# Perceiver block on one core: the shift of the context rows as tensor times scalar, the division of outputs moved next to the second clamp, GpSimd's first two key sums ahead of deviations

## The chip, the cores and the metric

The kernel runs on one core of one Trainium2 chip. The core has five engines with queues of their own: TensorE (PE in the profile; its weight loads are PEld), VectorE (DVE), ScalarE (ACT), GpSimd (POOL), and SyncE (SP), which here only issues transfers. They meet at semaphores. The metric is the device time of one execution in microseconds: 1367.38 us, the median of three runs of the kernel before (1366.13, 1367.38 and 1373.22 us).

## The reference, cut to what matters

The block takes 16 sequences of 64 latents of width 256 and a context of 1024 rows of width 256 for each sequence, and applies three residual layers. All is float32.

```
# 1. cross attention, 16 heads of 64:       what this case is about
ctx = layer_norm(context) * ln_ctx_g + ln_ctx_b
q = layer_norm(latents) @ Wq
k, v = split(ctx @ Wkv)                       # 1024 rows, 16 heads of 64
k = [k1 * cos - k2 * sin, k2 * cos + k1 * sin]
attn = softmax(clip(q k^T / 8, -11, 11))
x = x + (attn v) @ Wo + bo
# 2. causal linear attention with relu features, 3. eight experts, two for each token
x = x + linear_attention(layernorm(x))
x = x + experts(layernorm(x))
```

The change touches the first layer alone.

## The kernel before, in words

The cross attention works on 128 steps: 16 sequences by 8 steps, and a step `j` is half of one sequence's context (512 rows) against a pair of head pairs. `two_steps(j)` on VectorE and on TensorE issues two steps; four steps share one output, so that two calls make a cycle, called a quad here: a call with `j % 4 == 0` and one with `j % 4 == 2`. There are 32 quads. Every order is written out by hand; nothing is planned by a program.

TensorE, in a call for `j`: in every second call `outputs` (L1627, 64 small matmuls, into the banks that the keys use too), then `scores(j)` and `scores(j + 1)` (L1561, 64 small matmuls each), `keys(j + 4)` (L1575, 12 matmuls of 512 columns), `sums(j - 2)` (L1604, 12), `keys(j + 5)`, `sums(j - 1)`. `outputs` waits until VectorE has taken the last keys out of the banks (`ku_done`, 8 n + 24). `keys` waits for the same of the step before, `scores` for the finished keys of GpSimd (`kr_done`), `sums` for the low parts of the weights (`p_lo_done`).

VectorE, in a call: `blocks_turned` (L1077, a 32 by 32 transpose of context rows), `added` (L1090, every second call), `shifts(j)` (L1060), `counted(j)` (L1068 and L1070, mean and variance of a tile of context rows), `clamped(j)` (L1082, the clip of the exponentials), `keys_turned(j)` (two times L1114 and L1115: keys out of PSUM times sine and times cosine), `clamped(j + 1)`, `weights_low(j)` (L1102, `p_lo = pr - p_hi`), `blocks_turned(j)`, and in every second call `divided` (L1096, `qo = o_part * lsum`) and `inverted` (L1086), then `shifts(j + 1)`, `counted(j + 1)`, `keys_turned(j + 1)`, in every second call `half_low` (L1124), and `weights_low(j + 1)`.

GpSimd, in a step: `keys_summed(j)` (L593, the cosine part plus the swapped sine part, 128 x 1024 elements, both read from SBUF), `deviations(j)` (L601 and L603, the reciprocal standard deviation of a tile) and `rows_low(j)` (L609). `keys_summed(j)` waits for `p_lo_done` of step `j - 1`: it may start as VectorE ends that step's `weights_low`.

ScalarE exponentiates (L773), rounds (L778), copies `o_part` (L787) and applies `rstd` and `shift` to the context rows (L739). The swapped sine part `ksw` comes from `kw` by four transfers of SyncE (L448).

`shift` is a column of 128 numbers: minus the mean times the reciprocal deviation. Steps below 0 are the lead-in, written out call by call for VectorE and as a loop from -5 for GpSimd.

Of the kernel before, what the change touches and what calls it, by code (L numbers as in the profile page):

```python
# [20 lines left out]
ALU = mybir.AluOpType  # L21
# [39 lines left out]
def build(nc, x, ctx_1024, cos, sin, lat_g, lat_b, ctx_g, ctx_b, Wq, Wkv, Wo, bo, Wqkv, bqkv, Wout, bout, proj,  # L61
          Wg, W1, b1, W2, b2, out):
    with ExitStack() as ctx:
        def sem(name):
            return ctx.enter_context(nc.semaphore(name))

        def sb(name, shape, dt=F32, scope=ctx):
            return scope.enter_context(nc.sbuf_tensor(name, shape, dt))
# [9 lines left out]
        mv = sb("mv", [P, 2, 2])  # L78
        ve = sb("ve", [P, 2])
        rstd = sb("rstd", [P, 2])  # L80
        shift = sb("shift", [P, 2])
# [189 lines left out]
        stats_done, rstd_done, shift_done, xhat_done = (sem(n) for n in ("stats_done", "rstd_done", "shift_done", "xhat_done"))  # L271
# [12 lines left out]
        def wait(eng, s, count):  # L284

            if count > 0:
                eng.wait_ge(s, count)

        def there(j):
            return 0 <= j < STEPS  # L290

        def due(j, first):

            return j >= first and (j - first) % 4 == 0 and (j - first) // 4 < QUADS
# [32 lines left out]
        def kr_at(j):  # L327

            return (kr_third[:], kr[:, 0], kr[:, 1], kr_fourth[:])[j % 4]
# [21 lines left out]
        def quad_cols(n):  # L351

            return n // 2 * N, n % 2 * 4
# [202 lines left out]
        def _(pool):  # L556
# [30 lines left out]
            def keys_summed(j):  # L587
                if there(j + 2):
                    i = j % 2
                    pool.wait_ge(ku_done, 2 * (j + 3))  # L590
                    wait(pool, p_lo_done, j)
                    pool.wait_ge(sw_ld[i], ((j + 2) // 2 + 1) * 64)
                    pool.tensor_tensor(kr_at(j + 2), kr_at(j + 2), ksw[:, i], ALU.add).then_inc(kr_done, 1)  # L593
# [11 lines left out]
            def rows_low(j):  # L605
                if there(j + 4):
                    n, t = tile_at(j + 4)
                    pool.wait_ge(x_hi_done, j + 5)
                    pool.tensor_tensor(xc[:, n, 1, t, 0:D - 1], raw[:, (j + 4) // ST % 2, (j + 4) % ST, 0:D - 1], xc[:, n, 0, t, 0:D - 1].bitcast(F32),  # L609
                                       ALU.subtract).then_inc(x_lo_done, 1)  # L610
# [16 lines left out]
                pool.wait_ge(rstd_done, (2 * c + 1) * ST // 2)  # L627
                pool.tensor_tensor(xl_rsd[:, t], xl_vpe[:, t], consts[:, 2:3].to_broadcast([P, ST // 2]), ALU.pow).then_inc(rstd_done, ST // 2)
            constants()
            for j in range(-5, 0):  # L630
                deviations(j)
                rows_low(j)
                keys_summed(j)
            for j in range(STEPS):
                keys_summed(j)
                deviations(j)
# [378 lines left out]
        def _(dve):  # L1015
# [38 lines left out]
            def shifts(j):  # L1054
                for n in stats_at(j - 1):
                    i = n % 2
                    dve.wait_ge(rstd_done, 2 * (n + 1))
                    if n >= ST + 2:
                        dve.wait_ge(xhat_done, n - 1)
                    dve.scalar_tensor_tensor(out=shift[:, i:i + 1], in0=mv[:, i, 0:1], scalar=-1.0, in1=rstd[:, i:i + 1],  # L1060
                                             op0=ALU.mult, op1=ALU.mult).then_inc(shift_done, 1)

            def counted(j):
                for n in stats_at(j):
# [14 lines left out]
            def clamped(j):  # L1079
                if there(j):  # L1080
                    dve.wait_ge(exp_done, j + 1)
                    dve.tensor_scalar(step_part(pr, j), step_part(pr, j), LOW, HIGH, ALU.max, ALU.min).then_inc(clamp_done, 1)  # L1082
# [9 lines left out]
            def divided(n):  # L1092
                at, g = quad_cols(n)
                dve.wait_ge(o_sum, 2 * n + 2)
                dve.wait_ge(lsum_ld, 64 * n + 64)
                dve.tensor_tensor(qo[:, g:g + 4, at:at + N], o_part[:].rearrange("p (g n) -> p g n", n=N),  # L1096
                                  lsum[:].rearrange("p (g n) -> p g n", n=N), ALU.mult).then_inc(o_done, 1)

            def weights_low(j):
                if there(j):  # L1100
                    dve.wait_ge(p_hi_done, j + 1)
                    dve.tensor_tensor(step_part(p_lo, j), step_part(pr, j), step_part(p_hi, j).bitcast(F32), ALU.subtract).then_inc(p_lo_done, 1)  # L1102
# [23 lines left out]
            def two_steps(j):  # L1126
                blocks_turned(j - 1)
                if due(j, 8):
                    added((j - 8) // 4)
                shifts(j)  # L1130
                counted(j)
                clamped(j)
                keys_turned(j, 0)
                keys_turned(j, 1)
                clamped(j + 1)
                weights_low(j)
                blocks_turned(j)
                if due(j, 10):
                    divided((j - 10) // 4)
                if due(j + 1, 7):  # L1140
                    inverted((j - 6) // 4)
                shifts(j + 1)
                counted(j + 1)
                keys_turned(j + 1, 0)
                keys_turned(j + 1, 1)
                if half_written(j - 1):
                    half_low(half_written(j - 1))
                weights_low(j + 1)
# [171 lines left out]
            for j in range(0, STEPS, 2):  # L1320
# [10 lines left out]
                if j >= STEPS - 6:  # L1331
# [3 lines left out]
                    i = (j - STEPS + 6) // 2  # L1335
# [690 lines left out]
```

## Time and profile before

| | |
|---|---|
| time, median of three | 1367.38 us |
| the profiled execution | 1373.17 us, span of its instructions 1371.4 us |
| granted TensorE clock, mean | 0.954 of 2.4 GHz |
| busy: PE, DVE | 1231.1 us (90%), 1156.1 us (84%) |
| busy: ACT, POOL | 653.0 us (48%), 605.3 us (44%) |
| cross attention in steady state | 124 to 1016 us of the span, 27 quads |

The profiled execution is one of the slower ones. A row of the timeline begins with the start in us from the span's start and the duration; in square brackets stands how long the engine sat idle before it and what ended that. Busy time of an instruction runs from its start to its end, and holds any time in which it was held. Rows of a busy engine overlap a little, since the next instruction starts before the last has drained.

### The profile page before, as it was taken

What the parts mean: (1) busy time and instruction counts of PE and PEld (TensorE: products, weight loads), DVE (VectorE), ACT (ScalarE), POOL (GpSimd) and SP (SyncE); (2) the same over time, 40 slices, a digit from 0 to 9 for tenths busy, and PEclk for the clock granted to TensorE, in tenths of its full rate; (3) what the DMA queues carried; (4) which work ended last, traced back from release to release, by engine and by line L of the source; (5) the groups of instructions that cost most, each with busy time, mean ns of one, the idle gap of its engine ahead of it and who ended that gap; (6) DMA issues with size and microseconds to landing.
All of it is one profiled execution on the core that took longest, in us unless ns stands there. A gap on an engine that the chain in (4) does not pass through costs nothing.

```text
span 1371.4 us, 39825 instructions
## 1 busy us (share of the span) xinstructions
PE 1231.1 (90%) x16268; PEld 1036.8 (76%) x16268; DVE 1156.1 (84%) x1954; ACT 653.0 (48%) x1089; POOL 605.3 (44%) x611
## 2 busy tenths in 40 slices
PE   7888898988988989888898888988999999999997
PEld 3677777777767767767777777777778888789997
DVE  6799989998989998999889898888986736757886
ACT  7454444444444444444444444444544423346664
POOL 2455544454544444554444454444444313332333
PEclk9999999999999999999889898999999999999999
DMA  5365555555555555555456554555456371366662
GB/s 208 82 151 129 126 125 129 131 120 121 120 121 121 124 128 124 132 131 129 122 123 126 120 122 119 124 126 119 121 146 134 90 223 64 102 189 203 190 191 82
DMA packets 136173, 181.36 MB, mean 132 GB/s; under 512 B 30316, under 2 KB 96312, under 8 KB 135864
## 3 DMA queue, kind: packets, MB, share of 16 engines
q1 hardware_dynamic: 110552, 150.80, 43.4%
q10 hardware_dynamic: 21360, 23.80, 6.8%
q0 software_dynamic: 4080, 4.22, 1.5%
q8 instruction: 129, 2.11, 0.7%
q14 instruction: 52, 0.43, 0.1%
HBM read 81.93 MB, written 30.56 MB: 82 GB/s over the span
## 4 chain that ended last, share of the span: by engine, by line
DVE 49%; PE 39%; issue 7%; ACT 2%; DMA 2%; POOL 1%; SPq 0%; POOLq 0%; DVEq 0%; ACTq 0%
PE bank L1575 9%; DVE shift L1060 9%; DVE p_lo L1102 7%; PE bank L1561 7%; DVE kw L1114 6%; PE bank L1930 5%; DVE kr L1115 5%; DVE pr L1082 5%; DVE qo L1096 5%; PE bank L1627 4%; PE bank L1604 3%; DVE ct L1124 2%; DVE xt L1077 2%; DVE bst L1068 2%; DVE kr_fourth L1115 2%
## 5 line engine op out<-in xcount | busy, mean ns | idle before, releaser
L1575 PE MATMUL bank<-ct,wk_hi 128*128 128x512 f32 x1024 | 335.0, 409 | 5.9 <-DVE kr_third L1115 2.9
L1604 PE MATMUL bank<-p_hi,xc 128*128 128x512 f32 x1024 | 316.1, 390 | 0.0
L1575 PEld LDWEIGHTS bank<-ct,wk_hi 128*128 128x128 f32 x1024 | 190.0, 193 | 55.7 <-DVE kr L1115 8.7
L1114 DVE TENSOR_TENSOR kw<-bank,stab 128x512 f32<-128x512 f32 x256 | 175.3, 685 | 60.8 <-PE bank L1575 58.2
L1604 PEld LDWEIGHTS bank<-p_hi,xc 128*128 128x128 f32 x1024 | 191.9, 188 | 39.8
L593 POOL TENSOR_TENSOR kr<-kr,ksw 128x1024 f32<-128x1024 f32 x64 | 153.7, 2403 | 123.4 <-issue 120.5
L778 ACT CAST p_hi<-pr 128x1024 fp32r<-128x1024 f32 x128 | 134.3, 1049 | 150.4 <-DVE pr L1082 150.4
L1575 PE MATMUL bank<-ct,wk_lo 128*128 128x512 f32 x512 | 202.9, 396 | 0.0
L1604 PE MATMUL bank<-p_lo,xc 128*128 128x512 f32 x512 | 199.2, 389 | 0.0
L773 ACT ACTIVATE pr<-bank 128x1024 f32<-128x1024 f32 x128 | 127.8, 1026 | 81.6 <-PE bank L1561 81.5
L1060 DVE SCALAR_TENSOR_TENSOR shift<-mv,rstd 128x1 f32<-128x1 f32 x120 | 162.5, 1354 | 0.0
L1102 DVE TENSOR_TENSOR p_lo<-pr,p_hi 128x1024 fp32r<-128x1024 f32 x128 | 156.1, 1219 | 0.6 <-ACT p_hi L778 0.5
L609 POOL TENSOR_TENSOR xc<-raw,xc 128x255 fp32r<-128x255 f32 x128 | 95.1, 743 | 125.7 <-ACT xc L748 125.7
L1627 PE MATMUL bank<-zt,wv 64*64 64x64 f32 x2048 | 49.8, 265 | 93.3 <-DVE kr_fourth L1115 90.3
L739 ACT ACTIVATE raw<-raw,shift,rstd 128x256 f32<-128x256 f32 x120 | 71.8, 600 | 121.8 <-DVE shift L1060 121.7
L1627 PEld LDWEIGHTS bank<-zt,wv 64*64 64x64 f32 x2048 | 45.2, 174 | 105.7 <-issue 105.7
L1082 DVE TENSOR_SCALAR pr<-pr 128x1024 f32<-128x1024 f32 x128 | 102.8, 803 | 19.2 <-ACT pr L773 19.2
L593 POOL TENSOR_TENSOR kr_third<-kr_third,ksw 128x1024 f32<-128x1024 f32 x32 | 76.8, 2399 | 94.4 <-issue 88.2
L593 POOL TENSOR_TENSOR kr_fourth<-kr_fourth,ksw 128x1024 f32<-128x1024 f32 x32 | 77.9, 2434 | 87.7 <-issue 80.7
L1575 PEld LDWEIGHTS bank<-ct,wk_lo 128*128 128x128 f32 x512 | 98.4, 192 | 23.1 <-issue 0.9
L1604 PEld LDWEIGHTS bank<-p_lo,xc 128*128 128x128 f32 x512 | 96.1, 188 | 20.1
L1561 PE MATMUL bank<-qo,kr 64*64 64x64 f32 x4096 | 87.8, 239 | 17.2 <-issue 12.6
(227 smaller groups left out, 2190.8 us busy)
## 6 DMA issues: line engine op xcount, KB each, us to landing
ksw<-kw SPq DMA_DIRECT2D x512, 128.0 KB, 2.3
x_turned<-xt SPq DMA_DIRECT2D x120, 128.0 KB, 2.5
ct_read<-x_turned SPq DMA_DIRECT2D x30, 512.0 KB, 4.9
w_two<-in_L_ffn_W_dram SPq DMA_DIRECT2D x15, 1024.0 KB
raw<-in_ctx_dram ACTq DMA_DIRECT2D x56, 256.0 KB, 3.4
x_slots<-fill ACTq DMA_DIRECT2D x32, 258.0 KB, 3.3
w_all<-in_L_ffn_W_dram SPq DMA_DIRECT2D x4, 2048.0 KB, 17.0
wo<-in_L_ffn_W_dram SPq DMA_DIRECT2D x7, 1024.0 KB, 5.0
```

Source lines behind the costliest of these rows:

```text
L593: pool.tensor_tensor(kr_at(j + 2), kr_at(j + 2), ksw[:, i], ALU.add).then_inc(kr_done, 1)
L773: act.activation(step_part(pr, j).rearrange("p (t h c) -> p h t c", h=2, c=P), heads[j % 2].rearrange("p h (t c) -> p h t c", c=P), ACT.Ex ...
L778: act.copy(step_part(p_hi, j), step_part(pr, j)).then_inc(p_hi_done, 1)
L1060: dve.scalar_tensor_tensor(out=shift[:, i:i + 1], in0=mv[:, i, 0:1], scalar=-1.0, in1=rstd[:, i:i + 1], op0=ALU.mult, op1=ALU.mult).then_i ...
L1082: dve.tensor_scalar(step_part(pr, j), step_part(pr, j), LOW, HIGH, ALU.max, ALU.min).then_inc(clamp_done, 1)
L1102: dve.tensor_tensor(step_part(p_lo, j), step_part(pr, j), step_part(p_hi, j).bitcast(F32), ALU.subtract).then_inc(p_lo_done, 1)
L1114: dve.tensor_tensor(by_tile(kw[:, i, cols]), keys_, by_tile(stab[:, places]), ALU.mult).then_inc(kw_done, 1)
L1115: dve.tensor_tensor(by_tile(kr_at(j)[:, cols]), keys_, by_tile(ctab[:, places]), ALU.mult).then_inc(ku_done, 1)
L1561: last = pe.matmul(banks[c * N:(c + 1) * N, h, t * 2 + a], kr_at(j)[rows, cols], qo[rows, g, at:at + N], start=True, stop=True)
L1575: last = pe.matmul(psK[:, a * 512:(a + 1) * 512], l[:, k, w], ct[:, h % 3, r, k], start=(m == 0), stop=(m == len(parts) - 1))
L1604: last = pe.matmul(psZ[c], xc[:, slot_, l, t, cols], r[:, i, :, t], start=(f == 0 and m == 0), stop=(f == 1 and m == len(parts) - 1), skip ...
L1627: last = pe.matmul(out_bank(n, r)[h * DH:(h + 1) * DH, i * N:(i + 1) * N], wv[rows, k, g * P + h * DH:g * P + (h + 1) * DH], zt[rows, k, ( ...
```

## The change

Three edits. In `shifts`, the product of the mean, -1 and `rstd` is no longer one operation of two tensors and a constant but one of a tensor, a scalar read per partition (`rstd`) and a constant. In `two_steps` of VectorE, `divided` goes from behind `blocks_turned(j)` to between `clamped(j + 1)` and `weights_low(j)`. In GpSimd's lead-in, `keys_summed(-2)` and `keys_summed(-1)` go ahead of their step's `deviations` and `rows_low`.

```diff
             constants()
-            for j in range(-5, 0):
+            for j in range(-5, -2):
                 deviations(j)
                 rows_low(j)
-                keys_summed(j)
+            keys_summed(-2)
+            deviations(-2)
+            rows_low(-2)
+            keys_summed(-1)
+            deviations(-1)
+            rows_low(-1)
...
-                    dve.scalar_tensor_tensor(out=shift[:, i:i + 1], in0=mv[:, i, 0:1], scalar=-1.0, in1=rstd[:, i:i + 1],
-                                             op0=ALU.mult, op1=ALU.mult).then_inc(shift_done, 1)
+                    dve.tensor_scalar(shift[:, i:i + 1], mv[:, i, 0:1], rstd[:, i:i + 1], -1.0, ALU.mult, ALU.mult).then_inc(shift_done, 1)
...
                 clamped(j + 1)
+                if due(j, 10):
+                    divided((j - 10) // 4)
                 weights_low(j)
                 blocks_turned(j)
-                if due(j, 10):
-                    divided((j - 10) // 4)
                 if due(j + 1, 7):
                     inverted((j - 6) // 4)
```

The first place is VectorE in the second call of a quad, from the second clamp to the last keys of the quad. `pr` is clamped there, `p_lo` is the low part of the weights, `xt` the turned rows, `qo` the divided output, `kw` and `kr_fourth` the keys' sine and cosine parts. Before:

```order
L1082 TENSOR_SCALAR pr<-pr 128x1024
L1102 TENSOR_TENSOR p_lo<-pr,p_hi 128x1024
L1077 STREAM_TRANSPOSE xt<-raw 128x8x32
L1096 TENSOR_TENSOR qo<-o_part,lsum 128x4x64
L1086 RECIPROCAL l_parts<-l_parts 128x4
L1060 SCALAR_TENSOR_TENSOR shift<-mv,rstd 128x1
L1068 BN_STATS bst<-raw 128x6
L1070 BN_AGGR mv<-bst 128x2
L1114 TENSOR_TENSOR kw<-bank,stab 128x512
```

The same place after; the edits above have moved the line numbers by 4 or 5:

```order
L1086 TENSOR_SCALAR pr<-pr 128x1024
L1100 TENSOR_TENSOR qo<-o_part,lsum 128x4x64
L1106 TENSOR_TENSOR p_lo<-pr,p_hi 128x1024
L1081 STREAM_TRANSPOSE xt<-raw 128x8x32
L1090 RECIPROCAL l_parts<-l_parts 128x4
L1065 TENSOR_SCALAR shift<-mv,rstd 128x1
L1072 BN_STATS bst<-raw 128x6
L1074 BN_AGGR mv<-bst 128x2
L1118 TENSOR_TENSOR kw<-bank,stab 128x512
```

`qo` stands two rows earlier, ahead of `p_lo` instead of behind it, and `shift` is a TENSOR_SCALAR.

The second place is GpSimd in the lead-in, steps -2, -1 and the sum of step 0. `ve` and `rstd` are the deviations, `xc` the low rows, `kr_third` and `kr` the keys of steps 0, 1 and 2. Before:

```order
L601 TENSOR_TENSOR ve<-mv,consts 128x1
L603 TENSOR_TENSOR rstd<-ve,consts 128x1
L609 TENSOR_TENSOR xc<-raw,xc 128x255
L593 TENSOR_TENSOR kr_third<-kr_third,ksw 128x1024
L601 TENSOR_TENSOR ve<-mv,consts 128x1
L603 TENSOR_TENSOR rstd<-ve,consts 128x1
L601 TENSOR_TENSOR ve<-mv,consts 128x1
L603 TENSOR_TENSOR rstd<-ve,consts 128x1
L609 TENSOR_TENSOR xc<-raw,xc 128x255
L593 TENSOR_TENSOR kr<-kr,ksw 128x1024 x2
```

The same place after:

```order
L593 TENSOR_TENSOR kr_third<-kr_third,ksw 128x1024
L601 TENSOR_TENSOR ve<-mv,consts 128x1
L603 TENSOR_TENSOR rstd<-ve,consts 128x1
L609 TENSOR_TENSOR xc<-raw,xc 128x255
L593 TENSOR_TENSOR kr<-kr,ksw 128x1024
L601 TENSOR_TENSOR ve<-mv,consts 128x1
L603 TENSOR_TENSOR rstd<-ve,consts 128x1
L601 TENSOR_TENSOR ve<-mv,consts 128x1
L603 TENSOR_TENSOR rstd<-ve,consts 128x1
L609 TENSOR_TENSOR xc<-raw,xc 128x255
L593 TENSOR_TENSOR kr<-kr,ksw 128x1024
```

Each of the first two sums stands three and five rows earlier; the third keeps its place behind `xc`.

## Rows read from the trace of the kernel before

**Rows 1.** Busy time by stretch, us and instructions: PE, PEld, DVE, ACT, POOL; clock, DMA.

```profile
124.00:1016.00 892.00, 788.26 (x11232) 654.33 (x11225) 807.82 (x1181) 413.71 (x592) 431.41 (x426) 0.94 0.53 125
...
585.69:617.46 31.77, 27.70 (x416) 22.67 (x417) 30.43 (x45) 15.43 (x22) 16.14 (x16) 1.00 0.58 130
1016.00:1043.19 27.19, 27.19 (x416) 22.71 (x416) 22.59 (x29) 13.22 (x18) 13.14 (x8) 1.00 0.67 147
...
92.00:124.00 32.00, 25.65 (x233) 20.17 (x234) 31.86 (x44) 12.98 (x19) 16.96 (x16) 0.93 0.48 113
```

**Rows 2.** Waits of PE, 60 to 1010 us: total, times, longest; one in the timeline.

```profile
PE bank L1627 <- DVE kr_fourth L1115: 88.7, 26, 3.5
...
553.41 1.99 PE L1627 MATMUL bank<-zt,wv 64*64 64x64 f32 x64 [3.41 <-DVE kr_fourth L1115]
```

**Rows 3.** Timeline of DVE over one quad.

```profile
538.09 1.21 DVE L1102 TENSOR_TENSOR p_lo<-pr,p_hi 128x1024 fp32r<-128x1024 f32 x1
...
539.59 2.26 DVE L1060 SCALAR_TENSOR_TENSOR shift<-mv,rstd 128x1 f32<-128x1 f32 x1
...
542.32 0.66 DVE L1082 TENSOR_SCALAR pr<-pr 128x1024 f32<-128x1024 f32 x1
...
547.65 2.52 DVE L1096 TENSOR_TENSOR qo<-o_part,lsum 128x256 f32<-128x256 f32 x1
...
550.18 0.12 DVE L1060 SCALAR_TENSOR_TENSOR shift<-mv,rstd 128x1 f32<-128x1 f32 x1
...
556.20 0.71 DVE L1060 SCALAR_TENSOR_TENSOR shift<-mv,rstd 128x1 f32<-128x1 f32 x1
```

**Rows 4.** Timeline of POOL over the same quad.

```profile
539.44 2.40 POOL L593 TENSOR_TENSOR kr_third<-kr_third,ksw 128x1024 f32<-128x1024 f32 x1 [3.21 <-issue]
...
547.50 2.39 POOL L593 TENSOR_TENSOR kr<-kr,ksw 128x1024 f32<-128x1024 f32 x1 [1.81 <-issue]
...
554.53 2.36 POOL L593 TENSOR_TENSOR kr<-kr,ksw 128x1024 f32<-128x1024 f32 x1 [2.08 <-issue]
```

**Rows 5.** Groups by line, 124 to 1016 us: busy us, mean ns, idle before.

```profile
L1060 DVE SCALAR_TENSOR_TENSOR shift<-mv,rstd 128x1 f32<-128x1 f32 x106 | 147.9, 1396 | 0.0
...
L1096 DVE TENSOR_TENSOR qo<-o_part,lsum 128x256 f32<-128x256 f32 x27 | 68.1, 2521 | 0.0
...
L1077 DVE STREAM_TRANSPOSE xt<-raw 128x256 f32<-128x256 f32 x108 | 46.9, 435 | 0.0
...
L1068 DVE BATCH_NORM_STATS2 bst<-raw 128x6 f32<-128x256 f32 x105 | 43.5, 414 | 0.0
```

**Rows 6.** Timeline of POOL and of DVE from 118 us.

```profile
118.17 2.40 POOL L593 TENSOR_TENSOR kr<-kr,ksw 128x1024 f32<-128x1024 f32 x1 [1.82 <-issue]
...
118.33 0.13 DVE L1086 RECIPROCAL l_parts<-l_parts 128x4 f32<-128x4 f32 x1
118.38 2.20 DVE L1060 SCALAR_TENSOR_TENSOR shift<-mv,rstd 128x1 f32<-128x1 f32 x1
```

**Rows 7.** Timeline of DVE where the context rows have run out.

```profile
1003.66 2.80 DVE L1082 TENSOR_SCALAR pr<-pr 128x1024 f32<-128x1024 f32 x1
...
1038.68 0.41 DVE L1096 TENSOR_TENSOR qo<-o_part,lsum 128x256 f32<-128x256 f32 x1
```

**Rows 8.** Groups of the whole span: a scalar per partition, and a constant.

```profile
L1170 DVE TENSOR_SCALAR raw<-raw,xl_mom,xl_rsd 128x256 f32<-128x256 f32 x8 | 2.7, 405 | 0.3 <-POOL xl_rsd L628 0.3
...
L1027 DVE TENSOR_SCALAR crep<-cs_raw 128x256 f32<-128x256 f32 x8 | 1.7, 286 | 2.3 <-DMA cs_raw<-in_L_xattn_sin_dram 2.3
```

**Rows 9.** Timeline of the lead-in: POOL, DVE and PE.

```profile
48.97 2.41 POOL L593 TENSOR_TENSOR kr_third<-kr_third,ksw 128x1024 f32<-128x1024 f32 x1
...
57.12 5.11 POOL L593 TENSOR_TENSOR kr<-kr,ksw 128x1024 f32<-128x1024 f32 x2
...
58.17 1.84 DVE L1082 TENSOR_SCALAR pr<-pr 128x1024 f32<-128x1024 f32 x1
...
59.60 1.99 PE L1561 MATMUL bank<-qo,kr 64*64 64x64 f32 x64 [4.63 <-POOL kr L593]
```

## The prediction

> **What bounds the kernel now.** I read the table of stretches first, then the waits of TensorE, then the timelines of VectorE and GpSimd over one quad. The steady part, 124 to 1016 us, holds 27 quads in 892 us, 33.04 us each [rows 1]. TensorE is busy 788 us of it and VectorE 808 us, so neither looks free. But of VectorE's busy time much is no work. `shift` is 128 numbers, one for each partition, and takes 1396 ns in the mean; free of any hold it takes 0.12 us [rows 3, 5]. `qo` takes 2521 ns against 0.41 us when free [rows 5, 7]. The reader is to see what GpSimd does meanwhile: its 2.40 us sum starts at 539.44, just behind the end of `p_lo` (538.09 and 1.21), and `shift`, started at 539.59, ends at 541.85, with that sum [rows 3, 4]. `qo` from 547.65 to 550.17 sits on the sum of 547.50 to 549.89 in the same way. So VectorE is held, in a quad, 4 x 1.396 - 4 x 0.12 = 5.1 us in `shift` and 2.1 us in `qo`, 7.2 us of 33.04.
>
> TensorE pays for that in one place: `outputs` waits for the last keys of the quad (`kr_fourth`), 88.7 us in 26 waits, 3.41 us each [rows 2]. In the quad at 585.69, with the clock at full rate all through, 31.77 us minus that wait are 28.4 us of nearly unbroken work. The quad at 1016.00 shows TensorE with no wait at all: 27.19 us for the same 416 matmuls, clock 1.00 [rows 1]. The rest of the 33.04 us, 2.4 us, is clock and small stalls: a mean of 0.94 with the levels 2.4 and 1.2 GHz is 12% of the stretch, 107 us, at 1.2 GHz; if TensorE worked through all of it that costs 53 us, 2.0 us in a quad. Some quads with the 3.4 us wait run at 1.00, those without a wait at 1016 all do.
>
> **The change, part by part.** The shift first. Its new form reads one tensor and a scalar per partition. The trace has no such instruction under a key sum, so I bound it by its neighbours. Below: a reciprocal of one small input runs 0.13 us from 118.33, inside the sum that started at 118.17, and the old `shift` right behind it is held 2.20 us by that same sum [rows 6]; so what matters is not that VectorE works at all, but what the instruction reads. Above: the old hold, 1.396 us in the mean. A scalar per partition costs something of its own, 405 against 286 ns on 256 columns [rows 8], 0.12 us. I take the value of the nearest row, free, about 0.15 us.
>
> What is late next, for each of the four shifts of a quad? Behind the one at 539.59 comes 0.6 us of statistics and then the clamp (542.32), a tensor against constants over 1024 columns, and that form does get held: 2.80 us instead of 0.66 at 1003.66 [rows 3, 7]. So this hold moves to the clamp and only 0.5 us is won. Behind the two shifts of the odd steps come statistics (0.6 us) and four halves of keys out of PSUM (about 2.4 us), none of them held in the trace; they cover the 2.4 us sum whole. One of these two is won entirely, 2.1 us; the other was already short (0.12 at 550.18), since `qo` had absorbed the sum before it. The one at 556.20 had 0.59 us, and ScalarE's exponentials are waited for just behind it: nothing.
>
> The division: at its new place, behind the second clamp, no key sum runs (the last ended at 541.84, the next starts behind `p_lo`), so it takes 0.41 us, and 2.1 us go, as long as the shift behind it is free too. `p_lo` and the sum that it releases come 0.34 us later; that sum then lies beside transpose, statistics and keys. Its wait for `lsum` costs nothing: that transfer is issued two steps before. Together VectorE's chain gets 0.5 + 2.1 + 2.1 = 4.7 us shorter in a quad, 28.3 us instead of 33.04, and the 2.0 us of slow clock that it also waits behind leave it as well once TensorE has no gap: 26.3 us. That is below 27.19 us, so TensorE becomes the bound. A second way gives the same: in the quad at 1016.00 VectorE is busy 22.59 us, without transposes, shifts and statistics; four transposes (0.44), four statistics (0.41 and about 0.1) and four shifts (0.15) add 4.4 us: 27.0 us, in which holds of the clamps are counted as work [rows 1, 5, 7]. So the margin is between 0.2 and 2 us, thin but positive, and it is the weak point of this forecast.
>
> A quad then costs 27.19 us and some stalls. The clean quad at 585.69 had 1.2 us of them, the whole part on the mean 2.4 - 2.0 = 0.4 us; I take 0.65, 27.84 us. 27 x (33.04 - 27.84) = 140 us. Ends: no stall, 158 us; 1.2 us of stalls and a remaining gap of 1 us, 99 us.
>
> The lead-in: `scores(1)` waits 4.63 us for the second sum, which stands behind deviations and rows and starts at 57.12; the clamp at 58.17 is held by it to 60.0 [rows 9]. With the sums ahead, the first starts one step of deviation and rows before 48.97, an estimate of 46.5, the second behind it and one such step, at about 50.5 us, and ends before 54.97, when TensorE begins to wait: `scores(1)` starts there instead of at 59.60, and the keys behind it no longer start after a pause. I take 7 us, between 4.6 and 8. From there to the first `outputs`, TensorE is idle 6.35 us of 92 to 124, and its clock of 0.93 costs another 2.2 [rows 1]; some of that is a rescaling of weights that stays on VectorE. I take 7.5 us, between 3 and 9.
>
> Sum: 140 + 7 + 7.5 = 155 us. The span of 1371.4 us becomes 1216, and the profiled execution's 1373.2 becomes 1218. That execution is 5.8 us above the median of the three runs; from the median the same sum gives 1212. I say 1214 us.
>
> The Trainium skill, SBUF — State Buffer, section Who interferes with whom, says that VectorE with two inputs in SBUF, or in one of its two-port modes, and a GpSimd instruction that reads SBUF exclude each other for a whole instruction, and that one with at most one SBUF input outside these modes never waits; rows 3, 4 and 6 agree for two inputs and for one. The page also counts the tensor-times-scalar form among those that may enter a two-port mode, which speaks against the edit: by that the new shift would be held as before, and the rival below gets its chance from it.
>
> **The rivals.** First, the change doesn't do what it says: the per-partition scalar is fetched the way a second tensor is, or a tensor times scalar is held like the clamp at 1003.66. Then each shift still ends with the sum, and the 2.1 us of the division are paid back by the shift two rows behind it. Only the lead-in's 7 us remain: 1360 us. For it speaks row 1003.66; against it that 256 columns with per-partition scalars take 405 ns and with a constant 286, so this form is not the fast one that the clamp is, and one column leaves nothing to split.
>
> Second, VectorE stays the bound. The margin above is thin, GpSimd's `rows_low` (two SBUF inputs) can now lie in front of the last `p_lo` of a quad, and a gap that only shrinks leaves the slow clock behind it: 28.3 + 2.0 = 30.3 us a quad, 27 x 2.7 = 74 us, with 10 from the start 84: 1283 us.
>
> Third, the gaps go but TensorE's clock still falls to 1.2 GHz 12% of the time: 27.84 + 2.0 us, 27 x 3.2 = 86 us and 12 from the start: 1269 us. Against it: after 1016 us, with no waits, the clock is 1.00.
>
> Slower: the held shift of the first rival with the price of its new form on top, 0.12 us [rows 8] on 120 shifts, all on VectorE's chain, 14 us, with the early sums in the lead-in holding VectorE there and winning nothing: 1381 us. It decides from the point where the new shift is held in most odd steps.
>
> **How the numbers follow.** TensorE-bound quads 0.68, VectorE still the bound 0.12, slow clock without gaps 0.08, shift held 0.07, slower 0.03, something else 0.02. The likeliest gives 1214 us, its own range 1196 to 1245. With the third case and half of the second the range reaches to 1275; the low end is the stall-free quad with the better ends of the start. What a measurement of this kernel can tell from no change is about 0.5%, 7 us. The first rival, at 1360, lies on that border and counts half and half: faster 0.93, same 0.04, slower 0.03.
>
> **What the profile after would show.** Right: `shift` at 0.1 to 0.2 us in the mean over all 120; `qo` at 0.4; the wait of `outputs` for `kr_fourth` gone or under 0.5 us a quad; starts of `outputs` 27.5 to 28.3 us apart; clock above 0.98; VectorE with several short waits for TensorE's keys; the mean of the clamp up from 0.80 to about 1.2 us, since it takes over holds; the second key sum ended by 53 us. Wrong: `shift` still above 1 us (first rival or the slower case), or an `outputs` wait of 1 to 3 us with VectorE busy through the quad (second), or a clock of 0.94 with no waits (third).

## The result, and the profile after

The changed kernel takes 1234.12 us in the median of 4 runs (1229.36 to 1237.52), the kernel before 1367.43 on the same chip: ratio 0.9015, 95% interval 0.8973 to 0.9058. The forecast was 1214 us, with 1196 to 1245 us for its likeliest case and a range that reaches to 1275. The profiled execution took 1237.52 us, its span 1235.8, and the sum is again made there.

The stretches first, to be set beside [rows 1]; the columns are the same.

```profile
111.66:879.06 767.40, 743.72 (x11233) 618.73 (x11233) 685.61 (x1181) 411.75 (x592) 434.27 (x427) 0.99 0.59 146
...
479.45:506.65 27.20, 27.20 (x418) 22.71 (x417) 25.35 (x45) 15.28 (x22) 16.16 (x16) 1.00 0.62 153
506.65:535.67 29.02, 27.34 (x418) 22.72 (x417) 25.36 (x45) 15.44 (x22) 16.16 (x16) 1.00 0.55 142
```

The first block of `outputs` starts at 111.66 us (before: 123.65), the 28th at 879.06 (before: 1016.00). Between them lie the same 27 quads, now in 767.40 us instead of 892.35, 28.42 each instead of 33.05 (33.04 in [rows 1], where the stretch starts at 124.00). A clean quad takes 27.20 us, with TensorE busy in all of it; VectorE has 25.35 us of work there, so 1.85 us of slack. The account: 892.35 - 767.40 = 124.9 us from the quads, 12.0 from the start, and 1.3 lost behind the start of the 28th outputs (355.4 us before, 356.7 after): 135.6 us, which is 1371.4 - 1235.8.

What TensorE waits for in the steady part (total us, times, longest), against [rows 2], and the chain that ended last, by engine:

```profile
PE bank L1565 <- issue: 21.7, 14, 2.1
PE bank L1579 <- issue: 1.9, 2, 1.7
```

```profile
PE 87%; DVE 4%; issue 3%; DMA 2%; ACT 2%; SPq 1%; POOL 1%; POOLq 0%; ACTq 0%; DVEq 0%
```

The wait of `outputs` for `kr_fourth`, 88.7 us before, is gone. What is left has no releaser: "issue" is idle time for which the profile shows no other engine. The chain is TensorE's at 87%.

The two instructions that were changed, over the whole span (ns: shortest, median, longest), against [rows 5]:

```profile
L1065 DVE TENSOR_SCALAR shift<-mv,rstd x120: 164/174/216, 36.3 to 861.2; 128x1 f32<-128x1 f32 x120
```

```profile
L1100 DVE TENSOR_TENSOR qo<-o_part,lsum x32: 410/413/426, 133.4 to 971.5; 128x256 f32<-128x256 f32 x32
```

And VectorE beside GpSimd in one quad, first VectorE, then GpSimd, against [rows 3, 4]:

```profile
495.01 0.17 DVE L1065 TENSOR_SCALAR shift<-mv,rstd 128x1 f32<-128x1 f32 x1
...
495.81 1.99 DVE L1086 TENSOR_SCALAR pr<-pr 128x1024 f32<-128x1024 f32 x1
...
500.97 0.41 DVE L1100 TENSOR_TENSOR qo<-o_part,lsum 128x256 f32<-128x256 f32 x1
501.30 1.21 DVE L1106 TENSOR_TENSOR p_lo<-pr,p_hi 128x1024 fp32r<-128x1024 f32 x1
...
502.86 0.17 DVE L1065 TENSOR_SCALAR shift<-mv,rstd 128x1 f32<-128x1 f32 x1
```

```profile
494.86 2.39 POOL L593 TENSOR_TENSOR kr_third<-kr_third,ksw 128x1024 f32<-128x1024 f32 x1 [2.35 <-DVE p_lo L1106]
...
502.65 2.41 POOL L593 TENSOR_TENSOR kr<-kr,ksw 128x1024 f32<-128x1024 f32 x1 [2.15 <-issue]
```

The shift at 495.01 lies inside GpSimd's sum of 494.86 to 497.25 and takes 0.17 us. The clamp that comes 0.8 us later is held to 497.80, just past the end of that sum: the hold has moved on, as the prediction said. The shift at 502.86 lies under the next sum and is followed by statistics and keys, none of which is held: here the whole 2.1 us are won. `qo` at 500.97 stands clear of both sums.

The lead-in, against [rows 9], GpSimd and then TensorE:

```profile
47.23 2.40 POOL L593 TENSOR_TENSOR kr_third<-kr_third,ksw 128x1024 f32<-128x1024 f32 x1
...
51.08 2.87 POOL L593 TENSOR_TENSOR kr<-kr,ksw 128x1024 f32<-128x1024 f32 x1
```

```profile
54.55 1.16 PE L1565 MATMUL bank<-qo,kr_third 64*64 64x64 f32 x64
55.53 1.11 PE L1565 MATMUL bank<-qo,kr 64*64 64x64 f32 x64
```

The second sum ends at 53.95, and `scores(1)` starts at 55.53 straight behind `scores(0)`, instead of at 59.60.

### The profile page after: what moved, and what is told of

Read it like the earlier page. It is cut to its first block, busy times and chain, and to the rows that moved or that the text cites. A ratio compares the mean times of both kernels' runs of the same rounds, so it can differ in the third digit from the quotient of the medians.

```text
span 1235.8 us, 39825 instructions
## 1 busy us (share of the span) xinstructions
PE 1183.8 (96%) x16268; PEld 998.4 (81%) x16268; DVE 1021.3 (83%) x1954; ACT 650.5 (53%) x1089; POOL 609.2 (49%) x611
## 3 DMA queue, kind: packets, MB, share of 16 engines
q8 instruction: 129, 2.11, 0.7%
## 4 chain that ended last, share of the span: by engine, by line
PE 87%; DVE 4%; issue 3%; DMA 2%; ACT 2%; SPq 1%; POOL 1%; POOLq 0%; ACTq 0%; DVEq 0%
PE bank L1579 29%; PE bank L1608 27%; PE bank L1565 10%; PE bank L1934 6%; PE bank L1631 3%; PE bank L1738 2%; PE bank L1984 2%; PE bank L1985 2%; PE bank L1986 1%; PE bank L1791 1%; PE bank L1815 1%; PE bank L1834 1%; DMA x_slots<-xn_all,slot 1%; DMA w_two<-in_L_ffn_W_dram 1%; PE bank L1824 1%
## 5 line engine op out<-in xcount | busy, mean ns | idle before, releaser
L1579 PE MATMUL bank<-ct,wk_hi 128*128 128x512 f32 x1024 | 328.6, 402 | 5.3 <-DVE kr_third L1119 3.1
L1106 DVE TENSOR_TENSOR p_lo<-pr,p_hi 128x1024 fp32r<-128x1024 f32 x128 | 169.0, 1321 | 0.5 <-ACT p_hi L783 0.4
L1086 DVE TENSOR_SCALAR pr<-pr 128x1024 f32<-128x1024 f32 x128 | 140.0, 1094 | 20.1 <-ACT pr L778 18.1
L694 POOL DMA_INDIRECT out_dram<-ys,result_no x23 | 51.4, 2236 | 98.7 <-DMA out_dram<-ys,result_no 74.3
L1565 PE MATMUL bank<-qo,kr 64*64 64x64 f32 x4096 | 76.8, 220 | 22.6 <-issue 22.6
L1565 PEld LDWEIGHTS bank<-qo,kr 64*64 64x64 f32 x4096 | 68.0, 135 | 35.7 <-issue 35.7
L735 ACT COPY zt<-bank 128x512 f32<-128x512 f32 x64 | 37.2, 582 | 95.7 <-PE bank L1608 95.7
L1119 DVE TENSOR_TENSOR kr<-bank,ctab 128x512 f32<-128x512 f32 x128 | 86.8, 678 | 0.0
```

Of the source, the lines that this page charges most:

```text
L1119: dve.tensor_tensor(by_tile(kr_at(j)[:, cols]), keys_, by_tile(ctab[:, places]), ALU.mult).then_inc(ku_done, 1)
L1565: last = pe.matmul(banks[c * N:(c + 1) * N, h, t * 2 + a], kr_at(j)[rows, cols], qo[rows, g, at:at + N], start=True, stop=True)
L1579: last = pe.matmul(psK[:, a * 512:(a + 1) * 512], l[:, k, w], ct[:, h % 3, r, k], start=(m == 0), stop=(m == len(parts) - 1))
```

## The experiments

All ratios are to the kernel before, run on the same chip; starts, quads and waits come from one profiled execution of each kernel. The times of before there were 1365.23 us (first four kernels), 1368.96 (the next four), 1364.06 (three) and 1366.02 (the last).

**The parts of the change.** Four kernels carry it in pieces. Edit 1 is the shift's form, edit 2 the place of the division, edit 3 the order of GpSimd's first sums.

```diff
# edit 1
-                    dve.scalar_tensor_tensor(out=shift[:, i:i + 1], in0=mv[:, i, 0:1], scalar=-1.0, in1=rstd[:, i:i + 1],
-                                             op0=ALU.mult, op1=ALU.mult).then_inc(shift_done, 1)
+                    dve.tensor_scalar(shift[:, i:i + 1], mv[:, i, 0:1], rstd[:, i:i + 1], -1.0, ALU.mult, ALU.mult).then_inc(shift_done, 1)
# edit 2, in VectorE's two_steps(j)
                 clamped(j + 1)
+                if due(j, 10):
+                    divided((j - 10) // 4)
                 weights_low(j)
                 blocks_turned(j)
-                if due(j, 10):
-                    divided((j - 10) // 4)
# edit 3, GpSimd ahead of its loop
-            for j in range(-5, 0):
+            for j in range(-5, -2):
...
-                keys_summed(j)
+            keys_summed(-2)
...
+            keys_summed(-1)
```

Edit 1 alone:

> The kernel before with the new form of the shift alone. Theory (holds by GpSimd's key sum): shift falls to 0.15 us in the mean, but the division, which still stands behind p_lo, is held 2.1 us once a quad. VectorE's chain is 2.6 us a quad shorter, so a wait of outputs of 1 to 2 us stays and with it part of the slow clock: 30 us a quad, about 1280 us (1260 to 1300). Rival 1 (TensorE is the bound as soon as the shift is free, the division was covered): under 1245 us. Rival 2 (it takes both edits to win anything): above 1340 us.

Measured: 1286.14 us, 0.9404 (0.9372 to 0.9436), so 79 us of the change. The quads take 30.07 us (first outputs at 117.47, 28th at 929.25). The waits of TensorE from 124 to 900 us, and one `qo` of VectorE with GpSimd's sum beside it:

```profile
PE bank L1626 <- DVE kr_fourth L1114: 41.0, 25, 1.9
PE bank L1560 <- issue: 23.7, 14, 2.2
```

```profile
501.71 2.52 DVE L1095 TENSOR_TENSOR qo<-o_part,lsum 128x256 f32<-128x256 f32 x1
```

```profile
501.56 2.39 POOL L593 TENSOR_TENSOR kr<-kr,ksw 128x1024 f32<-128x1024 f32 x1 [1.82 <-issue]
```

`qo` is held to the end of that sum as before, and `outputs` still waits, 1.6 us a time instead of 3.4. So the free shift alone does not make TensorE the bound; it is the prediction's second rival, VectorE bound, come true for half the change. Its 30.3 us a quad are near the 30.07 by luck: the rival added 2.0 us for a slow clock that stays, but the granted clock of these 27 quads is 1.00, and what stands in its place are 24.6 us of issue waits, 0.9 a quad.

Edit 2 alone:

> The kernel before with the division moved alone. Theory: qo falls from 2.5 to 0.4 us, and the shift that now stands behind p_lo takes over the hold (from 0.12 to 2.2 us): no change, 1362 to 1372 us, mean of the shift up from 1.40 to 1.9 us. Rival (the division's own hold was the costly one): 2.1 us a quad less, 1305 us.

Measured: 1360.81 us, 0.9973 (0.9947 to 0.9998). The shift of its trace:

```profile
L1060 DVE SCALAR_TENSOR_TENSOR shift<-mv,rstd x120: 113/2201/2283, 36.2 to 979.7; 128x1 f32<-128x1 f32 x120
```

`qo` is free there (0.41 us), but the median shift is now held for 2.20 us: the hold that `qo` had absorbed falls on the next instruction that can be held. Edit 2 is worth 4 us alone, at the edge of what these runs tell from nothing. Together with edit 1 it is worth 49: without edit 3 the kernel gains 1368.96 - 1241.34 = 127.6 us, and edit 1 alone gave 79.1.

Edit 3 alone:

> The kernel before with GpSimd's first two sums ahead of their deviations. Theory: the wait of 4.6 us before the second scores goes, 5 to 7 us less: 1361 us. Rival (the wait only moves to the keys behind it): no change, 1367 us.

Measured: 1362.58 us, 0.9969 (0.9947 to 0.9991), first outputs at 120.06. The second scores start at 55.50 as in the changed kernel, 4.1 us sooner, but the first outputs only 3.6 us sooner. By the medians the edit gives 2.7 us, about half of the 5 to 7 that the theory expected; the rival's no change is ruled out only just.

Edits 2 and 3:

> The changed kernel with the old form of the shift. Theory: all that is left is the lead-in, since the old shift is held by each sum and takes over the division's hold: 1360 us. Rival (the division's place is worth 2.1 us a quad by itself): 1300 us.

Measured: 1358.47 us, 0.9938 (0.9914 to 0.9963): what edits 2 and 3 do without the first is 6.8 us. The rival, that the division does most of the work, falls.

Edits 1 and 2:

> The changed kernel with the first two key sums back behind the deviations; shift and division as changed. Theory: only the start is longer, by the 4 to 7 us by which the early sums moved the first scores: 1239 to 1243 us, first outputs at 116 to 119 us instead of 111.7. Rival (the late start is made up for by 124 us, since other work bounds the first steps): 1232 to 1236 us.

Measured: 1241.34 us, 0.9072 (0.9029 to 0.9116), 9.1 us above the changed kernel beside it. The spans of the two profiled executions differ by 7.6 us. First outputs at 116.73 against 111.16, so 5.6 of them lie in the start, as expected; 2.7 us are in the 27 quads (766.66 against 763.93 us), of about the size by which executions of one kernel differ.

The changed kernel itself, unaltered, on the two chips where the next kernels ran:

> The changed kernel unaltered, to stand beside the others on the same chip: 1229 to 1238 us, 0.90 of the kernel before.

Measured: 1232.24 us, 0.9005 (0.896 to 0.905).

> The changed kernel unaltered, beside the mixed order on the same chip: 1229 to 1238 us.

Measured: 1234.95 us, 0.9042 (0.9012 to 0.9072).

**Where the missing 0.6 us a quad went.** The clean quad takes 27.20 us, as forecast, but the mean one 28.42, so stalls cost 1.22 us and not 0.65. The stall in the changed kernel looks like this (TensorE, 422 to 427.5 us):

```profile
422.19 1.16 PE L1631 MATMUL bank<-zt,wv 64*64 64x64 f32 x64
423.17 1.11 PE L1565 MATMUL bank<-qo,kr_third 64*64 64x64 f32 x64
424.10 0.99 PE L1565 MATMUL bank<-qo,kr 64*64 64x64 f32 x55
426.62 0.35 PE L1565 MATMUL bank<-qo,kr 64*64 64x64 f32 x9 [1.52 <-issue]
```

A block of scores breaks off after 55 of its 64 matmuls, in the middle of work whose data are all there, for 1.5 us. Counted over TensorE's records, with weight loads and semaphore instructions, the stalled instructions have the numbers 3009, 3778, 6337, 8898, 9665, 11457 and so on: all 16 are 193 or 194 above a multiple of 256. The instruction queue moved 129 packets in the whole span, 2.11 MB, so 16 KB each; one of them lies in the 2.7 us around this stall (the DMA view of 424 to 426.7 us: packets, MB, share):

```profile
q8 instruction: 1, 0.02, 2.6%
```

That points to the fetch of instructions, in blocks of 256. The same count says which ends of blocks stall. Of the 89 in the 27 quads, 14 have at least 128 short matmuls, 256 instructions with their loads, in a row just before them, and all 14 stall, for 0.8 to 2.1 us. Another 54 fall earlier into a row of short matmuls, and none of them stalls. Of the 21 among long matmuls two do (0.25 and 1.7 us), both in the first keys behind a row of 192.

The test moves the instructions and leaves the work alone:

```diff
+            for _ in range(64):
+                pe.wait_ge(ident_done, 2)
             for j in range(2, STEPS - 4, 2):
                 two_steps(j)
```

> 64 waits on a semaphore that has long reached its value are put into TensorE's program ahead of the main loop; the work is unaltered. Theory (the stalls of 1.0 to 2.4 us inside TensorE's blocks of scores come from the fetch of its instructions, in packets of 16 KB for 256 instructions): every stall in the main loop moves 64 instructions, 32 matmuls, earlier in the work, and stays beside a 16 KB packet of the instruction queue; the ones that then fall into blocks of outputs or sums shrink, so the time changes by up to 1% either way: 1225 to 1245 us. Rival (the stalls belong to the data: a PSUM buffer, an operand that comes late): they stay at the same matmuls, and the time is the same within 0.3%.

Measured: 1236.64 us, 0.9033 (0.8991 to 0.9075). The same place in its trace:

```profile
422.98 1.16 PE L1631 MATMUL bank<-zt,wv 64*64 64x64 f32 x64
423.96 1.11 PE L1565 MATMUL bank<-qo,kr_third 64*64 64x64 f32 x64
424.89 0.76 PE L1565 MATMUL bank<-qo,kr 64*64 64x64 f32 x39
427.53 0.58 PE L1565 MATMUL bank<-qo,kr 64*64 64x64 f32 x25 [1.88 <-issue]
```

The stall now comes after 39 matmuls, 16 earlier. So it is wherever a stall stays inside the same row: stalls that stood at the matmuls 1469, 1846, 3106, 4365, 5625 and 6003 of the program stand at 1453, 1830, 3090, 4349, 5609 and 5987, at the same numbers of the instruction stream. The expectation said 32 matmuls; the 64 waits left only 32 more semaphore records, and 32 instructions are 16 pairs of load and matmul. The rival, stalls that belong to the data, falls. Some stalls vanish where they were (9665, 18113, 20674), and others appear or grow (5570, 8130, 16577, 25025), always as the count above has it: again the ends behind at least 128 short matmuls stall, 14 of 14, none of 54 earlier in a row, and one of 21 among long matmuls. So the total hardly moves: 22.1 us of issue waits in the 27 quads against 23.6.

The Trainium skill, Runtime: NRT & Kernel Launch, section Instruction fetch mechanics, says that an engine's instructions are fetched in blocks of 16 KiB, 256 instructions, while the current block runs, and that the price of crossing into the next block is mostly hidden. The size agrees with the numbers above. The price is hidden at 73 of the 89 ends in the steady part of the changed kernel; at the other 16 it shows as 0.25 to 2.1 us, 23.6 us in all, and the measurement decides.

Next, whether the order of the work decides if a fetch is late. TensorE's pair of steps in another order:

```diff
                 scores(j)
-                scores(j + 1)
                 if due(j, 8):
                     pe.wait_ge(o_sum, (j - 8) // 2 + 2)
                 keys(j + 4)
+                scores(j + 1)
                 sums(j - 2)
                 keys(j + 5)
                 sums(j - 1)
```

> TensorE's blocks of a pair of steps in another order: scores, keys, scores, sums, keys, sums instead of scores, scores, keys, sums, keys, sums. Theory (fetch of instructions falls behind where many short matmuls follow one another): with no two blocks of scores in a row the fetch has time to catch up, the stalls of 1.22 us a quad shrink to 0.4 to 0.8 us, 27 x 0.4 to 0.8 = 11 to 22 us: 1212 to 1224 us. Rival (a stall falls wherever a packet's end is met, whatever the order): 1229 to 1240 us. Other rival (VectorE, busy 25.35 of 27.20 us, now waits for keys or is waited for, since the two halves of keys come at other times): 1245 to 1280 us.

Measured: 1230.32 us, 0.8987 (0.8945 to 0.903); beside the changed kernel's 1232.24 that is no difference. Yet the stalls are gone. One of its quads, and TensorE's waits over all 27:

```profile
421.69:449.75 28.06, 28.04 (x418) 22.74 (x417) 25.04 (x45) 15.08 (x22) 18.21 (x17) 1.00 0.60 148
```

```profile
PE bank L1579 <- issue: 1.4, 2, 1.1
PE bank L1579 <- DVE o_part L1094: 0.3, 1, 0.3
```

The theory holds in its mechanism and fails in its sum. The quad without any stall takes 28.06 us here and not 27.20: two more rows of short matmuls stand between long ones in it, 0.43 us each. The expectation had no term for it.

So only the row of three short blocks, outputs and two scores, is broken up, in every second pair of steps:

```diff
                 scores(j)
-                scores(j + 1)
+                if not due(j, 8):
+                    scores(j + 1)
                 if due(j, 8):
                     pe.wait_ge(o_sum, (j - 8) // 2 + 2)
                 keys(j + 4)
+                if due(j, 8):
+                    scores(j + 1)
                 sums(j - 2)
```

> As the spread order, but only in the pairs of steps that begin with a block of outputs: outputs, scores, keys, scores, sums, keys, sums; the other pairs keep scores, scores, keys, sums, keys, sums. The trace of the spread order has quads of 28.07 us with no stall, 0.87 us over the clean 27.20 us for two more changes from short to long matmuls, 0.43 us each. Theory (the stalls come where outputs and two blocks of scores, 384 instructions of short matmuls, stand in a row): one more change, no stalls, quads of 27.63 us: 27 x 0.44 = 12 us under spread, 1216 to 1222 us. Rival (two blocks of scores in a row stall as well where a fetch is late): 1224 to 1232 us.

Measured: 1231.01 us, 0.9014 (0.8984 to 0.9044); beside it the changed kernel had 1234.95, and the intervals of the two ratios overlap. The 1216 to 1222 us of the theory are missed. TensorE's waits in the 27 quads, and VectorE at one of them:

```profile
PE bank L1579 <- DVE o_part L1094: 10.7, 24, 1.2
PE bank L1565 <- issue: 2.6, 2, 1.4
PE bank L1579 <- issue: 1.5, 1, 1.5
```

```profile
422.33 0.45 DVE L1081 STREAM_TRANSPOSE xt<-raw 128x256 f32<-128x256 f32 x1 [0.41 <-DMA x_turned<-xt]
422.70 0.39 DVE L1094 TENSOR_TENSOR o_part<-bank,o_part 128x256 f32<-128x256 f32 x1
```

The stalls are nearly gone as the theory said (4.1 us against 23.6), and the rival (two scores in a row stall as well) falls in the main, though two such stalls are left; but a new wait took their place, and the quads take 28.23 us in the mean. With one block of scores instead of two behind outputs, keys come to the bank before VectorE has added the two halves of outputs, and VectorE begins that sum late, behind a transpose that waits for a transfer. The last kernel moves the sum ahead of the transpose, on top of the mixed order:

```diff
-                blocks_turned(j - 1)
                 if due(j, 8):
                     added((j - 8) // 4)
+                blocks_turned(j - 1)
                 shifts(j)
```

> The mixed order of TensorE, and on VectorE the sum of the two halves of outputs ahead of the transpose that stood in front of it. In the mixed order the quads are free of stalls but take 28.06 us, not 27.63: keys wait 0.36 us for that sum (o_part), which VectorE begins at 422.70 behind a transpose that itself waits 0.41 us for a transfer, though ScalarE's half of it was there at 422.28. Theory (that wait is all that is missing): the sum ends by 422.70, keys start at once, quads of 27.65 us, 27 x 0.4 = 11 us less: 1216 to 1224 us. Rival (VectorE then waits for the same transfer behind the sum, and the 0.4 us come back at the clamp or at the keys): 1226 to 1234 us.

Measured: 1221.88 us (1218.34 to 1224.51, 6 runs), 0.8945 (0.8912 to 0.8979). Its 27 quads, and TensorE's waits in them:

```profile
111.06:862.43 751.37, 747.17 (x11233) 613.94 (x11233) 701.24 (x1181) 409.37 (x592) 447.99 (x427) 1.00 0.61 149
```

```profile
PE bank L1579 <- issue: 2.3, 2, 1.4
PE bank L1565 <- issue: 1.5, 1, 1.5
```

24 of the 27 quads take 27.66 to 27.74 us, the mean is 27.83, clock 1.00, 3.8 us of issue waits instead of 23.6. This version beats the kernel before by 10.5%, and by these medians it is 0.8 to 1.1% under the changed kernel: 1221.88 against 1232.24 to 1234.95 us. They were not run side by side; of the changed kernel's two intervals (0.896 to 0.905 and 0.9012 to 0.9072) the first overlaps with this one's upper end. Moving the sum in the changed kernel alone was not run; the waits of its TensorE have no row for that sum.

**What the hold depends on.** The prediction took the scalar per partition for a slower form than the constant, and drew from it that it is not held. The clamp allows a test on 1024 columns:

```diff
-            for c, v in ((2, -0.5), (3, EPS)):
+            for c, v in ((2, -0.5), (3, EPS), (4, LOW), (5, HIGH)):
...
-                    dve.tensor_scalar(step_part(pr, j), step_part(pr, j), LOW, HIGH, ALU.max, ALU.min).then_inc(clamp_done, 1)
+                    dve.tensor_scalar(step_part(pr, j), step_part(pr, j), consts[:, 4:5], consts[:, 5:6], ALU.max, ALU.min).then_inc(clamp_done, 1)
```

> The changed kernel with the clamp's two bounds read as scalars per partition from two columns, in place of constants. In the changed kernel the clamp takes 0.66 us free and 0.72 to 2.38 us in 58 cases beside a key sum of GpSimd, 1.09 us in the mean. Theory (what is held by the sum is the fast form of tensor against constants; scalars per partition leave that form, as 405 against 286 ns on 256 columns shows): no clamp is held, each takes 1.1 to 1.3 us, nearly the same, mean 1.15 to 1.25; VectorE has 1.8 us of slack a quad, so the time stays within 0.5% of the changed kernel. Rival (every tensor read and written in SBUF over many columns is held, whatever its bounds): it is held as before and longer, 1.5 to 1.8 us in the mean, VectorE becomes the bound, 1250 to 1290 us.

Measured: 1236.08 us, 0.9053 (0.9019 to 0.9088), as the changed kernel beside it. The clamp in its trace, and in the changed kernel's (shortest, median, longest, ns):

```profile
L1086 DVE TENSOR_SCALAR pr<-pr,consts x128: 782/928/2424, 57.5 to 949.5; 128x1024 f32<-128x1024 f32 x128
```

```profile
L1086 DVE TENSOR_SCALAR pr<-pr x128: 660/914/2382, 57.9 to 948.2; 128x1024 f32<-128x1024 f32 x128
```

My theory falls. Scalars per partition add 0.12 us to a free clamp and leave it as open to the hold as constants do; 58 clamps are held by a key sum in either trace. The 0.12 us are the same on 1024 columns as between the two rows of 256 columns [rows 8], so they are a fixed price and no sign of a slower form. The rival's mechanism is the right one, its price was too high: 1.17 us in the mean, VectorE did not become the bound. So the shift is not free because its scalars are per partition. What differs between it and the clamp is the one column against 1024; no run varied that alone, so it stays open where between them the hold begins. The Trainium skill, VectorE: DVE Perf Modes, section on the mode 2×_2P, says that this two-port mode splits a tensor along its outermost dimension longer than one. One column has none. By that, as I read it, the shift is outside the mode and the clamp inside with either kind of bound, and both traces agree, though neither shows the mode itself. Read so, the skill did not speak against the edit, as the prediction took it to.

## Why the prediction was right, and where it was off

**The shift, free at 0.15 us: right.** 0.174 us in the median, 0.216 at most; 110 of the 120 lie wholly inside a key sum. Of the two reasons given beside it the first (the form with scalars per partition is another one than the clamp's) was wrong, as the run with columns shows; the second, that one column leaves nothing to split, agrees with the traces and was not tested. The value came from the nearest row, the free reciprocal [rows 6], and that carried; so far as the forecast leaned on the first reason, it was luck.

**What is late next: right.** The hold goes to the clamp once a quad (1.99 us at 495.81). Its mean over all is 1.09 us, forecast about 1.2. Statistics and keys cover the sums of the odd steps whole. Two things the prediction did not name: a second clamp of the quad catches the end of a sum (0.82 us at 482.67), and GpSimd's `rows_low` holds a third (0.94 at 500.11).

**The division, 2.1 us a quad if the shift behind it is free: right, with its condition.** 2.1 x 27 = 57 us was the term; measured 49 on top of edit 1, and 4 without it. The difference is mostly that TensorE becomes the bound before all of it is used: with edit 1 alone `outputs` waited 43.4 us in the 27 quads, and with both edits they take 45.1 us less (811.78 and 766.66 us).

**VectorE's margin of 0.2 to 2 us: right, at its good end.** It has 25.35 us of work in a quad of 27.20, so 1.85 us. GpSimd's `rows_low` did hold a `p_lo` in each quad (1.72 against 1.21 us at 478.71 in the changed kernel's trace), which is inside that slack. The second rival has no place; edit 1 alone shows what it would have looked like.

**The clean quad of 27.19 us: right.** 27.20.

**The stalls, 0.65 us a quad: mis-sized, and the step that failed.** They cost 1.22 us, 27 x 0.57 = 15 us, three quarters of the 20 us between forecast and result. The prediction had both ends before it, 1.2 us from the quad at 585.69 and 0.4 from the mean, and chose between them near the mean. It also took slow clock (2.0 us) and stalls (0.4 us) off the old quad as two terms that have nothing to do with each other. The trace of the kernel before has, from 124 to 1016 us,

```profile
PE bank L1561 <- issue: 12.8, 12, 1.9
PE bank L1575 <- issue: 0.7, 1, 0.7
```

13.5 us in all, 0.5 a quad, against 23.6 us, 0.87 a quad, in the changed kernel, and mostly at the same places of the program. Two of its rows of short matmuls, and the stretch from each row's start to the end of its block of 256 instructions, show why (columns as in the table of stretches):

```profile
421.70 1.16 PE L1627 MATMUL bank<-zt,wv 64*64 64x64 f32 x64 [3.33 <-DVE kr_fourth L1115]
...
425.61 1.15 PE L1561 MATMUL bank<-qo,kr 64*64 64x64 f32 x60 [1.70 <-issue]
```

```profile
189.01 1.99 PE L1627 MATMUL bank<-zt,wv 64*64 64x64 f32 x64 [3.40 <-DVE kr_fourth L1115]
```

```profile
421.70:423.91 2.21, 2.21 (x132) 2.07 (x133) 1.93 (x4) 0.42 (x2) 1.09 (x1) 1.00 0.76 172
189.01:193.35 4.34, 4.34 (x152) 4.17 (x152) 2.91 (x6) 0.95 (x2) 2.55 (x2) 0.50 0.53 120
```

Both rows come behind the 3.4 us pause. The one at full clock reaches the end of its block in 2.21 us and then stalls for 1.70; the one at 1.2 GHz takes 4.34 us and does not stall. It is so in all four kernels that keep the pause (the one before and those with edit 2, edit 3, and both). Their quads have 56 ends of blocks behind at least 128 short matmuls. 17 came with the clock at 1.00 since the row's start: all 17 stall, 1.3 to 1.9 us, as long as in the changed kernel. 39 came with it at 0.50 for more than half of that time: 18 don't stall, and the mean over the 39 is 0.28 us. With edit 1 alone all 14 stall again, at clock 1.00. So it was not the pause that hid the stalls but the slow clock behind it: a slow row leaves the fetch more time. No run sets the clock by itself, but the same block ends stall at full clock and not, or little, at half (the one at 11457: 1.81 us in the kernel before, none with edit 2 alone). When the change gave the 2.0 us of clock back, it brought part of them back as stalls.

The rest of the 1.22 us is clock: in the steady part it fell to 1.2 GHz three times, at 340.5, 541.9 and 712.6 us, each time 0.7 to 1.6 us behind the end of a stall, and these are its three longest (2.0 to 2.1 us). A piece of the first of them beside a piece of what follows it, in the columns of the table of stretches:

```profile
340.50:343.50 3.00, 3.00 (x8) 2.33 (x9) 0.30 (x1) 3.00 (x5) 0.20 (x1) 0.50 0.40 143
344.00:347.00 3.00, 3.00 (x15) 2.45 (x14) 2.49 (x5) 1.78 (x3) 0.03 (x1) 1.00 0.32 103
```

8 matmuls begin in the one and 15 in the other, so about half the time is lost there; each fall lasts 3.4 us, which makes an estimate of 1.7 us each time, 5 us in three, 0.2 a quad. 0.87 and 0.2 make 1.07. The last 0.15 us, 4.2 in all, lie in the quads with a stall, which take 0.14 to 0.36 us more than 27.20, their wait and their clock together; the quads without one take 27.20, and the first 27.30.

**The clock comes back with the gaps: right.** 0.94 before, 0.99 after, and 1.00 already with edit 1 alone, where a wait of 1.6 us a quad is left; the third rival (a slow clock without gaps) has no place.

**The start, 14.5 us: 12.0.** The early sums start at 47.23 and 51.08 (forecast 46.5 and 50.5), the second ends at 53.95, before it is waited for. They moved the first outputs by 5.6 us, against 7 in the sum. The other 6.4 us (forecast 7.5) are mostly the shift's: edit 1 alone has the first outputs at 117.47, 6.2 us sooner than before.

**The tail** was not in the sum; it is 1.3 us longer.

## What to carry to other kernels

Ask of an instruction that is held what is the next one that can be held; two edits that each pass the hold on are worth little apart (79 and 4 us here) and much together (128). A stall measured in a kernel that also loses clock is a lower bound: take it from the rows at full clock (1.7 to 1.9 us in the kernel before, against 0.5 a quad in the mean), and don't add up slow clock and stalls as if they were independent. And when TensorE is the bound, its instruction stream is a resource too: keep long rows of short matmuls apart, but as few times as it takes, since every change from short to long has its price.

## What the runs showed of the hardware

- At full clock TensorE stalls where a block of 256 instructions ends behind at least 128 short matmuls (64x64, with their loads) in a row: 14 of 14 such ends in the changed kernel, 0.8 to 2.1 us, against 2 of the other 75. The stalls move with the instructions, not with the work.
- At a granted clock of 0.50 the same row is slower and the stall small or gone: 0.28 us in the mean of 39 such ends, against 1.6 us in 17 at full clock, in the four kernels that keep the long pause.
- Each further row of short matmuls between long ones costs 0.43 us: a clean quad takes 27.20 us with two such rows (the changed kernel), 27.67 with three (the last kernel, mixed order with the sum moved) and 28.06 with four (scores and keys by turns in every pair of steps).
- A `tensor_scalar` over 1024 columns is held by GpSimd's sum whether its bounds are constants or scalars per partition (0.66 and 0.78 us when free, up to 2.4 when held); the same operation on one column is not held (0.16 to 0.22 us).
- A `scalar_tensor_tensor` with two tensors is held by that sum even with one column (2.20 us in the median where `qo` is out of the way).
